# A graph layer, an attention over edges and four experts: one gather in 64 goes to another queue, and one pair is prepared a block earlier

## The chip, the cores and the metric

The kernel runs on one core of a Trainium2 chip. The core has engines with instruction streams of their own: TensorE (PE, with its weight load PEld), VectorE (DVE), ScalarE (ACT), GpSimd (POOL) and SyncE (SP). They order their work among each other by semaphores, which an instruction waits on and another raises. Data moves between HBM and the on-chip memory by DMAs, which POOL, SP and ACT issue. The metric is the device time of one execution in microseconds. The kernel before takes 6051.52 us (median of 3 runs, 6050.52 to 6075.12).

## The reference

Inputs are 12,500 nodes with 256 features, 200,000 edges sorted by their target, and a second list of 131,072 edges among 8,192 nodes that is not sorted. Two residual layers are computed, each on the normalised features:

```python
x = x + gnn(layernorm(x), src, dst, edge_weight, W, b)
x = x + ffn(layernorm(x)[None], W_gat, att_src, att_dst, b_gat,
            gamma, beta, W1, b1, W2, b2, edge_index)[0]

def gnn(features, src, dst, w, W, b):
    msgs = features[src] * w[:, None]
    agg = segment_sum(msgs, dst, num_segments=12500)      # dst is sorted
    return einsum('ni,oi->no', agg, W) + b

def ffn(x, ...):          # x: every node; 4 heads x 4 experts
    h = x @ W_gat
    alpha = softmax over the edges of each target (leaky_relu(a_src[src] + a_dst[dst]))
    scores = layernorm(segment_sum(h[src] * alpha) + b_gat).mean(heads)
    g = softmax of the two best experts' scores
    return sum over 4 experts of g[e] * (gelu(x @ W1[e] + b1[e]) @ W2[e] + b2[e])
```

The index lists are read on the chip; what depends on them (which step belongs to which tile) is worked out there.

## The kernel before

The program has three blocks, one after the other, with a barrier between them. The first (an opening, then `weighted_sums`) computes the first layer and ends near 3070 us. The second (`attention_and_experts`) runs the experts' products on TensorE while POOL and SP merge the sorted edges of the attention. The third combines the experts' results.

The change is in the first block, and at the seam to the second. In the first block the 200,000 edges lie as 1563 columns of 128 edges. Four columns are a **group** (GT = 4); there are 391 groups. The feature rows that the edges name are gathered from HBM into a **ring** of 16 slots (RING = 16), one group per slot, so that group g lies in slot g % 16. Sixteen groups are called a **round** here, r = g // 16; 24 rounds are full and seven groups are left over.

A gather is one indirect DMA of POOL, which brings one column: 128 rows of 1 KB (`gather`, line 692). The first 64 are issued in the opening (line 346, from the raw input). After that POOL runs through `refill(g)` for g = 16 to 390: it reads from `group_end` the step that ends group g - 16 (line 697), waits on `s_mm` until TensorE has done that step, and issues the four gathers of group g. POOL can so be at most 16 groups ahead of TensorE.

SP's loop (lines 673 to 676) waits for each slot until its four gathers have landed (`s_got[k]`, 16 per gather) and raises `s_ready`.

TensorE and VectorE work in **steps**, 488 in all, since a group whose edges belong to two output tiles is taken twice. VectorE makes four one-hot matrices of a step (`one_hots`: one TENSOR_SCALAR at line 916, four at line 920, each from the edges' targets and weights), two steps ahead of TensorE at most. TensorE waits for `s_hot` and `s_ready`, multiplies each with a gathered column into PSUM (`step`, line 861, four fp32 matmuls), and raises `s_mm`. When a step ends an output tile (98 tiles), TensorE also runs `stages` (lines 839 to 853), which with ScalarE takes the tile through W, the residual, the statistics and `W_gat`. Between the steps VectorE sorts the second edge list (for two thirds of the block), and TensorE counts and transposes for it.

Near the block's end VectorE computes the attention's node terms in two pieces: `terms(0)` for 88 tiles and `terms(1)` for the last ten, when all tiles are done.

In the second block the nodes are taken in 49 pairs of tiles. For a pair, ScalarE loads x (`load`, line 1276), VectorE normalises it (`normalise`, line 1421), TensorE transposes it (`turn`, line 1362), VectorE copies it out of PSUM (`out_of_psum`, line 1427), and then the experts' products start (line 1341). For pair 0 these stand in a row at the block's start.

Later in the second block SP fetches the attention's rows singly as well (line 1225, 80 bytes each), beside POOL's indirect gathers of the same table (line 1258).

## Time and profile before

| | |
|---|---|
| median of the runs (lowest, highest) | 6051.52 us (6050.52, 6075.12) |
| the profiled execution's own time | 6071.08 us |
| its span | 6069.4 us |
| TensorE busy | 3440.2 us (57% of the span) |
| POOL busy | 2688.8 us (44%) |
| VectorE busy | 2050.1 us (34%) |
| POOL's 1500 gathers of line 692 | 1432.4 us busy, 955 ns each |
| TensorE's 3904 matmuls of line 861 | 1171.9 us busy, 458 ns each |

The profile was taken in one execution; its own time is 0.3% above the median of the timed runs. "<-" in front of an engine and a name says what ended an idle time: a semaphore of that engine, a DMA, "remote" (a semaphore whose sender the profile doesn't resolve) or "issue" (the engine waited for nothing that the profile shows). PEclk is the clock that TensorE was granted, as a share of full speed.

### The profile page before, as it was taken

Reading aid. Unit: us, or ns where it says so; the run is one execution under the profiler, and the core shown is the slowest. Engines: PE = TensorE matmul, PEld = TensorE weight load, DVE = VectorE, ACT = ScalarE, POOL = GpSimd, SP = SyncE. Lnnn points to the kernel's source line nnn. Section 1 sums busy time; section 2 is a strip of 40 time slices with the busy share of each in tenths; the row PEclk is TensorE's granted clock in tenths of the full one; section 3 lists DMA queues with packets and bytes.
Section 4 is the critical chain, followed back from the end, with each engine's and each line's share of the span. In section 5 each row is a group of like instructions: output and inputs, shape, how many; then the busy total and the mean of one; then the engine's idle time right before and its main releaser. Section 6 shows DMA issues by size and latency. Waiting matters only on the chain. (4 is left out here: it accounts for less than half of the span.)

```text
span 6069.4 us, 66499 instructions
## 1 busy us (share of the span) xinstructions
PE 3440.2 (57%) x13893; PEld 2630.0 (43%) x13894; DVE 2050.1 (34%) x6854; ACT 818.5 (13%) x2321; POOL 2688.8 (44%) x2801
## 2 busy tenths in 40 slices
PE   1444535455556667677832224982928376389927
PEld 0333323333434545455621013871807255277826
DVE  5445454545453444423300000330303012033436
ACT  3100000000000111111200000220202011022216
POOL 4554545454444555555377774026070613420050
PEclk5666666676777777888955556995959688699968
DMA  7422222222222333333201101121111111111137
GB/s 236 130 81 64 74 61 73 70 75 66 73 64 77 91 89 95 89 96 96 71 15 10 13 11 20 60 78 14 56 14 40 28 35 43 19 50 44 55 124 304
DMA packets 281484, 425.60 MB, mean 70 GB/s; under 512 B 64296, under 2 KB 215091, under 8 KB 280243
## 3 DMA queue, kind: packets, MB, share of 16 engines
q0 software_dynamic: 113696, 216.93, 13.9%
q1 hardware_dynamic: 69567, 114.91, 5.2%
q10 hardware_dynamic: 98004, 91.50, 4.7%
q14 instruction: 157, 1.29, 0.1%
q8 instruction: 60, 0.98, 0.1%
HBM read 317.12 MB, written 105.98 MB: 70 GB/s over the span
## 5 line engine op out<-in xcount | busy, mean ns | idle before, releaser
L692 POOL DMA_INDIRECT rows<-feats,src_t x1500 | 1432.4, 955 | 1393.7 <-PE node_sums L861 817.6
L1258 POOL DMA_INDIRECT got<-row_dram,src_sorted x1008 | 995.4, 988 | 1313.0 <-DMA state_dram<-got 1005.1
L861 PE MATMUL node_sums<-rows,ys_ahead 128*128 x3904 | 1171.9, 458 | 709.8 <-issue 548.7
L861 PEld LDWEIGHTS node_sums<-rows,ys_ahead 128*128 128x128 f32 x3904 | 859.0, 230 | 992.7 <-issue 856.0
L1352 PE MATMUL d_expert<-w,hid 128*128 128x256 f32 x3136 | 806.3, 398 | 557.8 <-issue 553.2
L1341 PE MATMUL d_hidden<-d_yt,w 128*128 128x256 f32 x3136 | 807.6, 399 | 525.6 <-issue 518.9
L1352 PEld LDWEIGHTS d_expert<-w,hid 128*128 128x128 f32 x3136 | 624.9, 199 | 710.6 <-issue 629.2
L1341 PEld LDWEIGHTS d_hidden<-d_yt,w 128*128 128x128 f32 x3136 | 622.8, 200 | 676.9 <-issue 600.4
L1404 DVE TENSOR_TENSOR yo<-d_expert,x_and_b 128x512 f32<-128x512 f32 x196 | 135.6, 692 | 2169.4 <-remote 1124.4
L1285 ACT ACTIVATE hid<-d_hidden,b1c 128x256 f32<-128x256 f32 x784 | 324.0, 471 | 2312.4 <-remote 1091.6
L920 DVE TENSOR_SCALAR ys_ahead<-iota,rel,ew_t 128x128 f32<-128x128 f32 x1952 | 566.7, 361 | 117.9 <-issue 50.1
L916 DVE TENSOR_SCALAR rel<-dst_t,step_base 128x4 f32 x488 | 118.0, 242 | 1182.5 <-remote 597.8
L1038 DVE TENSOR_SCALAR ys_ahead<-iota_b,hist_columns 128x128 bf16<-128x128 bf16 (+1 forms) x2048 | 348.4, 267 | 106.2 <-issue 97.6
L751 ACT COPY edge_plan<-node_sums 128x256 f32<-128x256 f32 x98 | 36.5, 372 | 2555.9 <-remote 1700.1
L873 PE MATMUL counts<-ys_ahead 128*128 128x98 bf16 x1024 | 80.5, 251 | 254.4 <-DVEq L1041 184.5
L873 PEld LDWEIGHTS counts<-ys_ahead 128*128 128x128 bf16 x1024 | 68.8, 123 | 267.5 <-DVEq L1041 191.4
L1265 POOL DMA_INDIRECT first_row<-state_dram,first_end x1 | 0.9, 942 | 330.2 <-DMA state_dram<-got 330.2
L502 POOL DMA_INDIRECT adst_first<-node_dst,first_pos x98 | 96.0, 980 | 107.6 <-DVEq L1082 68.9
L1757 PE MATMUL f_sum<-ys,gate_diagonals 128*128 128x256 f32 x384 | 95.6, 413 | 75.1 <-issue 75.1
L849 PE MATMUL x_product<-edge_plan 128*128 128x256 f32 x400 | 129.2, 455 | 0.0
L833 PE MATMUL node_sums<-b_zeros 1*128 1x256 bf16 x198 | 59.3, 300 | 120.5 <-issue 105.9
L1757 PEld LDWEIGHTS f_sum<-ys,gate_diagonals 128*128 128x128 f32 x384 | 79.1, 209 | 91.2 <-issue 78.7
(303 smaller groups left out, 2473.2 us busy)
## 6 DMA issues: line engine op xcount, KB each, us to landing
y_dram<-yo ACTq DMA_DIRECT2D x196, 256.0 KB
ys<-y_dram SPq DMA_DIRECT2D x36, 1024.0 KB
got<-row_dram SPq DMA_DIRECT2D x2048, 0.1 KB
rows<-feats,src_t POOLq DMA_INDIRECT x1500
got<-row_dram,src_sorted POOLq DMA_INDIRECT x1008
ys_ahead<-y_dram SPq DMA_DIRECT2D x13, 1024.0 KB
x_dram<-edge_plan ACTq DMA_DIRECT2D x98, 128.0 KB
d_x<-x_dram ACTq DMA_DIRECT2D x49, 256.0 KB
```

The lines of the kernel that those rows point to most:

```text
L692: pool.indirect_dma_start(rows[:, g % RING, j, :], None, feats, bass.IndirectOffsetOnAxis(ap=m.src_t[:, g * GT + j:g * GT + j + 1], axis=0 ...
L849: t = pe.matmul(psX[:, 0:FEAT], sums_t[:, k * P:(k + 1) * P], w_t[:, k, :], start=False, stop=(k == HALVES - 1))
L861: t = pe.matmul(psA[:, ds(((code >> 1) & 1) * 512, FEAT)], hot[:, r, j, :], rows[:, ds((code >> 2) & (RING - 1), 1), j, :], start=False, s ...
L873: t = pe.matmul(psC[:, 0:TILES], hot_lo[:, q % 2, j, :], hot_hi[:, q % 2, j, :], start=False, stop=False)
L920: t = v.tensor_scalar(hot[:, r, j, :], m.iota[:], rel[:, r, j:j + 1], m.ew_t[:, ds(g * GT + j, 1)], ALU.is_equal, ALU.mult)
L1038: c.inc(v.tensor_scalar(t[:, q % 2, j, :], iota_b[:, 0:wide], col[:, q % 2, n, j:j + 1], None, ALU.is_equal))
L1258: pool.indirect_dma_start(got[:, k, j, 0:ROWF], None, m.row_dram, bass.IndirectOffsetOnAxis(ap=m.src_sorted[:, BEGIN[b] + j:BEGIN[b] + j + ...
L1285: t = act.activation(hid[:, e % 2, 2 * q + f, :], psL[(e % 2) * 2 + q][:, f, :], ACT.Gelu, bias=b1c[:, e, 2 * q + f:2 * q + f + 1])
L1341: t = pe.matmul(psL[(e % 2) * 2 + q][:, f, :], w1[:, h, e, (2 * q + f) * P:(2 * q + f + 1) * P], yt[:, k, h, :], start=(h == 0), stop=(h = ...
L1352: q = pe.matmul(psO[e % 2][:, t, :], hid[:, e % 2, f, t * P:(t + 1) * P], w2[:, f, e, :], start=(f == 0), stop=(f == FB - 1))
L1404: v.tensor_tensor(yo[:, e, :, :], psO[e % 2][:], xb[:, e, :, :], ALU.add).then_inc(s_yo, 1)
L1757: q = pe.matmul(psum[j % SUMS][:, t, :], diag[:, j % DIAGS, t, e, :], y_of(i)[:, t, e, :], start=(e == 0), stop=(e == EXPERTS - 1))
```

## The change

There are two edits.

**Rows.** In rounds 2 to 23, the fourth column (`ROW_COL` = 3) of slot 15 (`ROW_SLOT`) isn't gathered by POOL. SP loads that column's 128 node numbers and fetches the 128 rows one by one: ten after the ready signal of each slot from 2 to 13, and eight at slot 14. At slot 15 SP waits until all have landed. So that SP may write into the slot, POOL waits once a round, ahead of `refill(16r + 3)`, until TensorE has done group 16r - 1, and raises `s_free` (`row_slot_free`). `by_row` picks the group: with g = 16r + 3, g + 16 - 2 - 2 is 16r + 15.

**First pair.** x of pair 0 is loaded by ScalarE ahead of its work for tile 97, normalised by VectorE between `terms(0)` and `terms(1)`, transposed by TensorE after the first of the four closing stages and copied by VectorE. In the second block `load(0, 0)`, `normalise(0, 0)`, `turn(0)` and `out_of_psum(0, 0)` are gone, and the waits on their semaphores count one less.

```diff
+ROW_SLOT, ROW_COL, ROW_FROM, ROWS_A_GROUP = 15, 3, 2, 10
...
+        m.x_first, m.y_first = m.ys_ahead[:, HI_SLOT, 0, 0:2, :], m.ys_ahead[:, HI_SLOT, 0, 2:4, :]
+        m.yt_first = m.ys_ahead[:, HI_SLOT, 1, 0:2, :]
...
@@ weighted_sums, SP
+            def ask_nodes(i):
+                sp.dma_start(node_row_of, src_cols[ds(i * (RING * GT) + (ROW_SLOT * GT + ROW_COL), 1), :]
+                             ).then_inc(s_wr, 16)
+
+            def single_rows(a, z):
+                _, nodes = nc.values_load_multi_w_load_instructions(
+                    node_row_of[0:1, a:z], engines=[mybir.EngineType.SP], min_val=0, max_val=NODES - 1,
+                    skip_runtime_bounds_check_because="edge_index names nodes")
+                for n, node in enumerate(nodes):
+                    sp.dma_start(rows[a + n:a + n + 1, ROW_SLOT, ROW_COL, :], feats[ds(node, 1), :]
+                                 ).then_inc(s_rows, 16)
+
+            sp.wait_ge(s_wr, 16)
             with sp.Fori(2, full_rounds) as i:
+                ask_nodes(i)
                 for k in range(RING):
-                    sp.wait_ge(s_got[k], i * (16 * GT) + 16 * GT)
+                    if k == ROW_SLOT:
+                        sp.wait_ge(s_got[k], i * (16 * (GT - 1)) + (16 * GT + 16))
+                        sp.sem_inc(s_past, 1)
+                        sp.wait_ge(s_rows, i * (16 * P) - 16 * P)
+                    else:
+                        sp.wait_ge(s_got[k], i * (16 * GT) + 16 * GT)
                     sp.sem_inc(s_ready, 1)
+                    if k == ROW_FROM:
+                        sp.wait_ge(s_free, i)
+                        sp.sem_inc(s_past, 1)
+                        sp.wait_ge(s_wr, i * 16)
+                        sp.sem_inc(s_past, 1)
+                    a = (k - ROW_FROM) * ROWS_A_GROUP
+                    if 0 <= a < P:
+                        single_rows(a, min(a + ROWS_A_GROUP, P))
...
@@ weighted_sums, POOL
+            def by_row(g):
+                return g % RING == ROW_SLOT and 2 <= g // RING < full_rounds
+
             def gather(g):
                 for j in range(GT):
+                    if j == ROW_COL and by_row(g):
+                        continue
...
+            def row_slot_free(g):
+                end = pool.value_load(m.group_end[0:1, g - RING:g - RING + 1], min_val=1, max_val=STEPS)
+                pool.wait_ge(s_mm, end)
+                pool.sem_inc(s_free, 1)
...
             for g in range(RING, GROUPS):
+                if by_row(g + RING - ROW_FROM - 2):
+                    row_slot_free(g + RING - ROW_FROM - 2)
                 refill(g)
...
@@ weighted_sums, ScalarE
+                if j == TILES - 1:
+                    act.wait_ge(s_x1o[0], 16)
+                    act.wait_ge(s_x1o[1], 16)
+                    act.wait_ge(s_pos, 1)
+                    act.dma_start(m.x_first, m.x1_dram.rearrange("(t p) f -> t p f", p=P)[:, 0:2, :]
+                                  ).then_inc(s_xin, 16)
                 tile(j, j % XS)
...
@@ weighted_sums, TensorE: after stages(TILES)
+                    pe.wait_ge(s_turn, PIECES - 8)
+                    for t in range(2):
+                        for h in range(HALVES):
+                            q = pe.transpose(psT[:, h * N2 + t * P:h * N2 + (t + 1) * P],
+                                             m.y_first[:, t, h * P:(h + 1) * P], m.ident[:])
...
@@ weighted_sums, VectorE: after terms(0)
+                    v.wait_ge(s_xin, 16 * TILES + 16)
+                    for t in range(2):
+                        c.inc(v.tensor_scalar(m.y_first[:, t, :], m.x_first[:, t, :], m.mean[:, t:t + 1],
+                                              m.rstd[:, t:t + 1], ALU.subtract, ALU.mult))
...
+                    c.done(v.tensor_copy(m.yt_first, psT[:, 0:HALVES * N2].rearrange("p (h n) -> p h n", n=N2)))
...
@@ attention_and_experts
-            load(0, 0)
...
-            turn(0)
...
-            normalise(0, 0)
-            out_of_psum(0, 0)
```

On POOL, the place is the seam from group 34 to group 35 (the fourth group of round 2). Before, every group is one load of its `group_end`, one wait on TensorE's steps and four gathers:

```order
107 L697 TENSOR_LOAD group_end
108 L697 ISA x2
109 L692 DMA rows<-feats,src_t 128x256 [waits b_step_multiplied]
110 L692 DMA rows<-feats,src_t 128x256 x3
111 L697 TENSOR_LOAD group_end
112 L697 ISA x2
113 L692 DMA rows<-feats,src_t 128x256 [waits b_step_multiplied]
114 L692 DMA rows<-feats,src_t 128x256 x3
```

And in the changed kernel at the same place:

```order
107 L742 TENSOR_LOAD group_end
108 L742 ISA x2
109 L732 DMA rows<-feats,src_t 128x256 [waits b_step_multiplied]
110 L732 DMA rows<-feats,src_t 128x256 x3
111 L737 TENSOR_LOAD group_end
112 L737 ISA x2
113 L742 TENSOR_LOAD group_end [waits b_step_multiplied]
114 L742 ISA x2
115 L732 DMA rows<-feats,src_t 128x256 [waits b_step_multiplied]
116 L732 DMA rows<-feats,src_t 128x256 x3
```

A second load of `group_end` (line 737) and a wait now stand ahead of group 35's own. The second wait is for an earlier step than the first, and everything that POOL does later stands behind the first.

On SP, the place is the start of its loop over the rounds. Before, the loop body holds only waits and register work (the waits of all 16 slots are gathered into one row here, which is left out):

```order
54 L672 DMA state_dram<-edge_plan 128x24
55 L673 UNCONDITIONAL_BRANCH
56 L673 ISA
```

In the changed kernel it begins with the load of 128 node numbers, and from the third slot on each row is one instruction (ISA) that forms the address and one DMA:

```order
55 L694 UNCONDITIONAL_BRANCH [waits b_w_and_row_nodes_loaded]
56 L694 ISA
57 L682 DMA edge_plan<-in_src 1x128
58 L702 REGISTER_ALU
59 L707 REGISTER_ALU [waits rows_gathered0,rows_gathered1,rows_gathered2,x_cleared_then_row_slot_free]
60 L686 TENSOR_LOAD edge_plan [waits b_w_and_row_nodes_loaded]
61 L690 ISA
62 L690 DMA rows<-feats 1x256
63 L690 ISA
64 L690 DMA rows<-feats 1x256
```

SP's first row of a round stands behind the ready signals of slots 0 to 2 and behind POOL's signal `x_cleared_then_row_slot_free`; the ready signal of slot 3 stands behind ten rows.

On TensorE, the place is the seam of the blocks. Before, the second block opens with the transposes of pair 0:

```order
5313 L518 UNCONDITIONAL_BRANCH
5314 L1330 UNCONDITIONAL_BRANCH [waits barrier_Pool_Activation_PE_DVE_SP_release]
5315 L1362 MATMUL d_y_turned<-ident,d_y 128x128 [waits d_normed]
5316 L1362 MATMUL d_y_turned<-ident,d_y 128x128 x3
5317 L1341 MATMUL d_hidden<-d_yt,w 128x256 [waits d_yt_ready]
5318 L1341 MATMUL d_hidden<-d_yt,w 128x256 x15
```

In the changed kernel the transposes stand in the first block, between two of the closing stages, and the second block opens with the products:

```order
5301 L906 MATMUL sums_and_xc_turned<-ident,edge_plan 128x128 x2
5302 L964 MATMUL turned<-ident,ys_ahead 128x128 [waits b_turn_ask]
5303 L964 MATMUL turned<-ident,ys_ahead 128x128 x3
5304 L892 MATMUL h_product<-wg,edge_plan 128x16 [waits b_tile_out_of_psum]
...
5315 L521 UNCONDITIONAL_BRANCH
5316 L1398 UNCONDITIONAL_BRANCH [waits barrier_Pool_Activation_PE_DVE_SP_release]
5317 L1410 MATMUL d_hidden<-ys_ahead,w 128x256 x16
```

The experts' first products no longer wait for a transpose in their own block; the second of the closing stages stands behind a wait on VectorE.

## Rows read from the trace of the kernel before

**Rows 1.** Page, part 5: costliest groups in the first block (columns as the page's head says).
```profile
L692 POOL DMA_INDIRECT rows<-feats,src_t x1500 | 1432.4, 955 | 1393.7 <-PE node_sums L861 817.6
...
L861 PE MATMUL node_sums<-rows,ys_ahead 128*128 x3904 | 1171.9, 458 | 709.8 <-issue 548.7
```

**Rows 2.** Waits, whole span: engine, line, releaser: total us, times, longest us.
```profile
POOL rows L692 <- PE node_sums L861: 817.6, 96, 38.0
...
PE node_sums L861 <- issue: 548.7, 205, 13.3
...
PE node_sums L861 <- SPq L676: 27.6, 9, 3.8
```

**Rows 3.** Stretches of the first block: us; PE, PEld, DVE, ACT, POOL busy (instructions); PEclk; DMA; GB/s.
```profile
352.00:1936.00 1584.00, 799.96 (x3400) 582.75 (x3398) 790.75 (x3367) 72.75 (x290) 738.02 (x777) 0.69 0.24 70
1936.00:2958.00 1022.00, 729.01 (x2750) 521.86 (x2749) 391.43 (x1193) 144.29 (x580) 583.72 (x609) 0.83 0.32 93
2959.00:3028.00 69.00, 69.00 (x311) 52.48 (x312) 32.56 (x106) 18.50 (x74) 0.44 (x1) 0.96 0.10 30
```

**Rows 4.** One stretch, line 861 alone, then line 833 alone: PE, PEld, PEclk, DMA, GB/s.
```profile
2959.00:3028.00 69.00, 39.11 (x171) 32.05 (x172) 0.96 0.10 30
...
2959.00:3028.00 69.00, 4.28 (x15) 1.36 (x15) 0.96 0.10 30
```

**Rows 5.** POOL's timeline in one run of gathers: start, duration, line, [idle before <-releaser].
```profile
501.34 0.94 POOL L692 DMA_INDIRECT rows<-feats,src_t  x1 [26.40 <-PE node_sums L861]
502.58 0.97 POOL L692 DMA_INDIRECT rows<-feats,src_t  x1 [0.30 <-issue]
...
520.08 0.95 POOL L692 DMA_INDIRECT rows<-feats,src_t  x1 [0.31 <-issue]
```

**Rows 6.** Stretches within that run, all engines: columns as in rows 3.
```profile
501.00:508.00 7.00, 6.53 (x31) 5.40 (x29) 4.27 (x16) 0.00 (x0) 5.14 (x6) 1.00 0.28 78
508.00:521.00 13.00, 4.36 (x10) 2.35 (x8) 1.47 (x5) 0.00 (x0) 9.96 (x11) 0.61 0.39 110
```

**Rows 7.** Stretches in the opening: first gathers of the long run, the rest, behind it.
```profile
20.00:35.00 15.00, 5.55 (x25) 3.99 (x23) 14.30 (x53) 10.28 (x22) 11.35 (x12) 0.73 1.09 350
35.00:106.00 71.00, 5.64 (x8) 2.14 (x8) 16.45 (x63) 8.93 (x19) 48.78 (x51) 0.52 0.68 219
99.30:106.00 6.70, 0.00 (x0) 0.00 (x0) 2.93 (x9) 0.00 (x0) 0.00 (x0) 0.50 0.13 42
107.00:122.00 15.00, 0.00 (x0) 0.00 (x0) 14.48 (x76) 12.76 (x30) 0.00 (x0) 0.50 0.54 168
```

**Rows 8.** Stretches in the second block: start of a run of gathers, its rest, and without gathers.
```profile
4047.00:4062.00 15.00, 15.00 (x71) 13.19 (x71) 3.58 (x7) 1.68 (x4) 11.34 (x13) 1.00 0.84 315
4062.00:4235.00 173.00, 35.98 (x67) 17.61 (x65) 3.73 (x8) 3.36 (x8) 118.70 (x126) 0.52 0.11 12
4250.00:4350.00 100.00, 100.00 (x473) 88.05 (x472) 33.92 (x68) 29.27 (x61) 0.00 (x0) 1.00 0.15 50
```

**Rows 9.** SP's timeline in the second block, single rows: start, duration of all, count.
```profile
5634.29 134.34 SPq L1225 DMA_DIRECT2D got<-row_dram  x256
```

**Rows 10.** The same, beside POOL's gathers.
```profile
3149.92 179.90 SPq L1225 DMA_DIRECT2D got<-row_dram  x42
```

**Rows 11.** Timeline at the seam of the first two blocks.
```profile
3068.06 0.30 ACT L805 ACTIVATE std_all<-rstd_all,eps 128x10 f32<-128x10 f32 x1
...
3073.22 0.92 ACTq L1276 DMA_DIRECT2D d_x<-x_dram  x2
...
3076.11 0.73 DVE L1421 TENSOR_SCALAR d_y<-d_x,mean,rstd_all 128x256 f32<-128x256 f32 x2 [4.80 <-DMA d_x<-x_dram]
...
3076.90 1.11 PE L1362 MATMUL d_y_turned<-ident,d_y 128*128 128x128 f32 x4 [13.12 <-DVE d_y L1421]
...
3078.05 0.69 DVE L1427 COPY d_yt<-d_y_turned 128x512 f32<-128x512 f32 x1 [1.21 <-PE d_y_turned L1362]
...
3078.80 5.49 PE L1341 MATMUL d_hidden<-d_yt,w 128*128 128x256 f32 x12 [0.78 <-issue]
```

More of the change, by code:

```diff
@@ L169, in build @@
             opening = layernorm_and_plan(nc, sem, x, src, dst, edge_weight, feats, m)
-            weighted_sums(nc, sem, opening, feats, edge_index, x, W, b, W_gat, att_src, att_dst, W1, b1, W2, b2, m)
+            weighted_sums(nc, sem, opening, feats, src, edge_index, x, W, b, W_gat, att_src, att_dst, W1, b1, W2, b2, m)
         attention_and_experts(nc, sem, m)
@@ L503, in spread, with weighted_sums @@
                             m.node_dst[:, t, :], None).then_inc(m.s_sc, 16)
-def weighted_sums(nc, sem, opening, feats, edge_index, x, W, b, W_gat, att_src, att_dst, W1, b1, W2, b2, m):
+def weighted_sums(nc, sem, opening, feats, src, edge_index, x, W, b, W_gat, att_src, att_dst, W1, b1, W2, b2, m):
     XS = 4
@@ L571, in weighted_sums @@
         zeros = lent(512)
+        node_row_of = lent(P)[0:1, :].bitcast(I32)
         std = sb("std_all", [P, TILES])
@@ L585, in weighted_sums @@
         s_pc = sem("b_pool_const")
-        s_wr = sem("b_w_loaded")
+        s_wr = sem("b_w_and_row_nodes_loaded")
+        s_free, s_rows = m.s_clear, sem("b_rows_landed")
         s_w, s_wt, s_wte = sem("b_weights"), sem("b_w_turned"), sem("b_w_ready")
@@ L906, in _ @@
                 stages(d)
+                if d == TILES:
+                    pe.wait_ge(s_turn, PIECES - 8)
[3 more added lines that the diff above has]
+                                             m.y_first[:, t, h * P:(h + 1) * P], m.ident[:])
+                    q.then_inc(s_turned, 1)
         @block.vector
@@ L1333, in layer1 @@
             def layer1(i, k, n, e, first=False):
-                if e == 0:
-                    pe.wait_ge(s_yt, i + 1)
+                turned = m.yt_first if isinstance(i, int) and i == 0 else yt[:, k]
+                if e == 0 and not (isinstance(i, int) and i == 0):
+                    pe.wait_ge(s_yt, i)
                 for q in range(2):
@@ L1356, in turn @@
             def turn(i):
-                pe.wait_ge(s_yn, i + 1)
-                if not isinstance(i, int) or i >= 1:
-                    pe.wait_ge(s_yt, i)
+                pe.wait_ge(s_yn, i)
+                if not isinstance(i, int) or i >= 2:
+                    pe.wait_ge(s_yt, i - 1)
                 for t in range(2):
@@ L1410, in x_and_b2 @@
                 bias = b2p[:, e, :] if e < IN_PSUM else b2r[:, e, :]
-                v.tensor_tensor(xb[:, e, 0, :], xd[:, k, 0, :], bias, ALU.add).then_inc(s_xh, 1)
+                of = m.x_first if isinstance(i, int) and i == 0 else xd[:, k]
+                v.tensor_tensor(xb[:, e, 0, :], of[:, 0, :], bias, ALU.add).then_inc(s_xh, 1)
                 v.wait_ge(s_xh, i * EXPERTS + (e + 1))
-                v.tensor_tensor(xb[:, e, 1, :], xd[:, k, 1, :], bias, ALU.add).then_inc(s_xb, 1)
+                v.tensor_tensor(xb[:, e, 1, :], of[:, 1, :], bias, ALU.add).then_inc(s_xb, 1)
             def normalise(i, k):
-                v.wait_ge(s_x[k], (i // 2) * 16 + 16 if isinstance(i, int) else i * 8 + (16 - 8 * k))
-                if not isinstance(i, int) or i >= 1:
-                    v.wait_ge(s_ty, i)
+                v.wait_ge(s_x[k], (i // 2) * 16 + 16 * k if isinstance(i, int) else i * 8 + 8 * k)
+                if not isinstance(i, int) or i >= 2:
+                    v.wait_ge(s_ty, i - 1)
                 for t in range(2):
```

12 lines of the change are left out of this document (9 added, 3 removed).

## The prediction

> **What bounds the kernel now.** I read the page's costliest groups first. POOL's gathers of the first block take 1432.4 us, and POOL is idle nearly as long before them, most of it released by TensorE's matmul of line 861 [rows 1]. The table of waits says the same from both sides: POOL waits 817.6 us for TensorE, TensorE only 27.6 us for SP's ready signal, in nine waits [rows 2]. So POOL is ahead by the whole ring, and the rows that it fetches are in time. The wait row to look at is TensorE's "issue": 548.7 us in 205 pieces of up to 13.3 us [rows 2], in which nothing that the profile shows holds it. The question is what does.
>
> The answer is in the stretches around POOL's runs of gathers. In one run POOL starts 16 gathers from 501.34 to 520.08, one every 18.74 / 15 = 1.25 us [rows 5]. In the first 7 us of it the other engines issue 31 + 29 + 16 instructions; in the 13 us after that, with the gathers still running, 10 + 8 + 5 [rows 6]. That is 10.9 per us against 1.8. The opening's long run has it too: after its first dozen gathers, 8 + 8 + 63 + 19 = 98 instructions come in 71 us (1.4 per us), and TensorE has none in the 6.7 us after the last gather; then VectorE alone issues 76 in 15 us [rows 7]. In the second block, TensorE has 71 matmuls in the first 15 us of such a run (the whole of which it is busy), then 67 in 173 us, and 473 in 100 us without gathers [rows 8]. Granted clock and issue fall together there (1.00 to 0.52), but half the clock can't explain a seventh of the instructions. So I read: a run of gathers back to back leaves the other engines alone for about 8 gathers (10 us), then slows all of them to 0.86 (148 in 173 us, rows 8) to 1.8 instructions per us until some 7 us after its end. Short runs cost little; long ones cost nearly their whole length.
>
> In this sense the ring's fullness before is a good thing: since POOL is always 16 groups ahead, it gets a slot only when TensorE has done a group, and its runs stay at 8 to 16 gathers by my count along its timeline, of which rows 5 are one.
>
> **The change, part by part.**
>
> *Fewer gathers.* 22 of 1500 gathers go; 22 x 1.25 = 27 us less for POOL, which waits 817.6 us anyway [rows 1, 2]. By itself I count this as nothing to at most 27 us.
>
> *POOL's new wait.* Ahead of group 16r + 3 POOL waits until TensorE has done group 16r - 1. Its own wait there is for group 16r - 13. So once a round POOL's lead falls from 13 to 16 groups to three (16r to 16r + 2). Behind the waiting instruction stand all of POOL's later gathers; SP's ready signals stand behind these. Once TensorE is there, the slots of groups 16r + 3 to 16r + 15 are free together: 13 x 4 - 1 = 51 gathers without a wait, and 12 more (the next three groups) that want TensorE to have done 16r to 16r + 2. POOL then runs 63 gathers in one go, 63 x 1.25 = 78.7 us, where before 64 came in four to six runs. With the 6.7 us behind it [rows 7] this is 85.4 us.
>
> How far does TensorE get in them? The instructions per group come from the two parts of the block: 777 gathers are 194 groups, with (3400 + 3398 + 3367 + 290) / 194 = 54 instructions on the four engines; later, when the sort is over, 609 are 152 groups, with 7272 / 152 = 48 [rows 3]. In the first 10 us it runs undisturbed, 2.1 groups at the pace below. In the remaining 69 us to the last gather I take 0.86 per us, the nearest row that had SP's single rows beside it: 59 instructions, 1.1 groups. Together 3.2 groups, just what it takes for POOL to issue its last 12 gathers without a stop. The bounds: nothing in the slow part (2.1 groups), or 1.8 per us (2.5 groups, 4.6 together).
>
> The undisturbed pace is read where POOL has gathered its last: from 2959 to 3028 line 861 has 171 records; 3904 over 488 steps are 8 a step, so 21.4 steps. Line 833 has 15, two a tile, so 7.5 tiles end there, each of which makes one step more than there are groups: 13.9 groups [rows 1, 4]. Of the 69 us I take off 7 for the run's tail: 62 / 13.9 = 4.46 us per group late in the block. Early on there are 54 instructions instead of 48 for each: an estimate of 5.0 us, above VectorE's 790.75 / 194 = 4.1 us of work per group [rows 3].
>
> A round after the change is then 85.4 + 12.8 x 5.0 = 149.4 us early and 85.4 + 12.8 x 4.46 = 142.5 us late. Before it is 1584 / 777 x 64 = 130.5 and 1022 / 609 x 64 = 107.4 [rows 3]. Rounds 2 to 13 lie in the early part, 14 to 23 in the late one: 12 x 18.9 + 10 x 35.1 = 227 + 351 = +578 us. As a test of the rule, a round before with some 33 us of slow time in it gives 33 + 16 x 4.46 = 104 late (107.4 measured), and 113 early (130.5): early it may be 17 us too kind.
>
> *SP's rows.* Without gathers beside it SP issues 256 single rows in 134.34 us, 0.525 us each [rows 9]; beside them 42 in 179.90 us, 0.23 per us [rows 10]. The rows here are 1 KB and not 80 bytes, which no row of before shows. In the first 10 us of a run some 15 rows go out, in 69 us at 0.23 another 16; the 97 left take 51 us in the quiet part, which has 57 (late) to 64 us (early). So they are hidden, by a little; the ready signal of slot 15 is the first to be late if a row costs over 0.66 us (64 / 97) early, or 0.59 late. I take nothing here and keep the dearer case as a rival. Below nothing it can't be: these are instructions added.
>
> *The first pair.* At the seam ScalarE's load is issued at 3073.22, VectorE normalises at 3076.11, TensorE transposes at 3076.90 and its products start at 3078.80 [rows 11]. Without these four steps the products could start when the load did, 5.6 us earlier. Against it the closing stages wait for two normalisations and four transposes (0.73 + 1.11 us in rows 11), beside work that ends at 3068.06. Between +3 and -6 us; I take -5.
>
> The sum: 578 - 5 = +573, on the profiled execution's 6071 us 6644. That execution was 20 us above the median of the runs, so I forecast 6051.5 + 573 = 6625 us.
>
> **Bounds of the likeliest case.** With 4.6 groups in the run, rounds of 11.4 groups: 142.4 and 136.2, 12 x 11.9 + 10 x 28.8 = +431, 6480. With 2.1 groups: 154.9 and 147.4, +693, 6740; and with the 17 us that the early rounds lacked, 6740 + 204 = 6940. I take 6350 to 6900 as its own range.
>
> **Rivals.**
>
> 1. *Slow, but in shorter runs.* TensorE hasn't done group 16r when POOL has issued 51 gathers; POOL stops, and the last 12 go out four at a time, as before. A round is 51 x 1.25 + 6.7 = 70.5 us with three groups, and 13 groups: 135.5 and 128.5, 12 x 5.0 + 10 x 21.1 = +271: 6320, down to 6100 if the pause sets in earlier. For it: 3.2 groups are near. Against it: two of the three groups it asks for are done in the undisturbed 10 us. 0.10.
>
> 2. *Dearer: SP's rows are the bound.* If a 1 KB row costs 0.8 us when quiet, 97 take 78 us, and a round is 85 + 78 = 163: 12 x 32.5 + 10 x 55.6 = +946, 7000. It decides from 0.6 us a row. Against it: rows 9. 0.07.
>
> 3. *No change.* The gathers and the slow stretches only happen to fall together, POOL's 4 x 1.25 = 5.0 us per group stay below TensorE's 107.4 / 16 = 6.7 us, and a lead of three groups is enough. Then only the first pair counts: 6046. For it: POOL waits 817.6 us. Against it: three stretches of different kinds show the same fall [rows 6 to 8]. 0.06. The Trainium skill (SBUF — State Buffer, Who interferes with whom) would have this one: it says that only the port pair that VectorE and GpSimd share makes engines wait for each other, so that TensorE would go on beside any run of gathers. TensorE's 67 matmuls in 173 us beside gathers against 473 in 100 us without [rows 8] speak against that rule, whatever the carrier.
>
> 4. *Faster.* One long run per round leaves a long quiet stretch; place: TensorE's pace between POOL's runs. It decides by how many groups TensorE does in the 85.4 us: the round is shorter than before from 16 - (130.5 - 85.4) / 5.0 = 7.0 groups early, and 16 - (107.4 - 85.4) / 4.46 = 11.1 late. With one group more than that in each round, 12 x 5.0 + 10 x 4.5 = 105 us are gained: 5945. For it: nothing but that the short runs, too, have a slow part each. Against it: TensorE would need two to three times what rows 6 show. 0.06.
>
> **How the numbers follow.** The forecast has 0.71, the rivals 0.10, 0.07, 0.06 and 0.06. The range 6130 to 6900 leaves out rivals 2 to 4 (0.19). A measurement of this kernel can tell about 0.5% (30 us) from no change: faster 0.06, the same 0.06, slower 0.88.
>
> **What would show it.** In the profile after, POOL's timeline in rounds 2 to 23 has runs of about 60 gathers and then an idle time of some 60 us that TensorE's matmul ends; before the change the longest of these was 38.0 us [rows 2]. TensorE's and VectorE's "issue" waits grow by some hundreds of us, PEclk in the first block falls, and the block ends near 3640 us instead of 3070, with the second and third as long as before. The first-pair step is right if the experts' products start within some 2 us of ScalarE's first work in their block. The forecast is wrong if TensorE's pace within POOL's long runs is like that outside of them, or if it is TensorE's wait on SP's ready signal that has grown.

## The result, and the profile after

The changed kernel takes 6998.04 us (median of 4 runs, 6990.66 to 7002.02), the kernel before 6058.89 us on the same chip: a ratio of 1.155 (95% interval 1.1528 to 1.1573), 939 us more. The forecast was 6625 us in a range of 6130 to 6900. The direction was right; the size was not, and the time lies outside the range.

The whole difference is in the first block. By the times at which TensorE finishes groups (my own count from its matmuls), round 23 ends at 3930.8 us instead of 3002.2 and round 1 ends 29 us earlier than before (323.2, 352.0). From the experts' first products to the end it is 2990.5 us, as before (2990.6). The page after, its line of engines and the two groups that answer to [rows 1]:

```profile
PE 3482.9 (50%) x13893; PEld 2631.6 (38%) x13894; DVE 2034.7 (29%) x6854; ACT 819.6 (12%) x2321; POOL 2659.6 (38%) x2779
...
L732 POOL DMA_INDIRECT rows<-feats,src_t x1478 | 1410.3, 954 | 2327.1 <-issue 2049.3
L914 PE MATMUL node_sums<-rows,ys_ahead 128*128 x3904 | 1220.7, 469 | 1438.9 <-issue 610.1
```

Busy times are nearly as before; what has grown is idle time. TensorE is busy 43 us longer, at a lower granted clock (0.64 and 0.70 in the stretches below, 0.69 and 0.83 in [rows 3]), so the clock is a small part of the 939 us. The table of waits, to be read beside [rows 2]:

```profile
POOL rows L732 <- issue: 2049.3, 1455, 95.9
...
PE node_sums L914 <- issue: 610.1, 198, 40.3
PE node_sums L914 <- remote: 353.8, 18, 39.9
PE node_sums L914 <- SPq L703: 352.4, 88, 26.4
```

Three things are to be seen. POOL's waits are put down to "issue", since the second load of `group_end` now stands between the wait and the gather; its 21 pieces above 10 us, 1612 us together and up to 95.9 us long, are the new wait (own count); the rest are the short gaps between gathers. TensorE's pieces of "issue" are up to 40.3 us long instead of 13.3. And there is a wait that was almost absent: TensorE for SP's ready signal, 352.4 us in 88 pieces instead of 27.6 us in nine. Of the 353.8 us whose sender the profile doesn't resolve ("remote"), 306 us end with an update of the same ready semaphore (own count), so the wait is nearer 650 us.

Rounds 2 to 13 and 14 to 23, from round end to round end, all engines (columns as in [rows 3]):

```profile
323.20:2312.50 1989.30, 790.20 (x3399) 574.74 (x3398) 786.93 (x3365) 74.16 (x295) 721.45 (x756) 0.64 0.19 55
2312.50:3930.80 1618.30, 836.94 (x2943) 573.79 (x2942) 397.15 (x1258) 155.07 (x622) 615.57 (x646) 0.70 0.22 64
```

The 756 gathers are 12 x 63. A round takes 1989.3 / 12 = 165.8 us early and 1618.3 / 10 = 161.8 us late; by the same marks it took 132.0 and 106.7 before. So +33.8 and +55.1 us, 12 and 10 times: 957 us. Early and late rounds are now nearly as long as each other, although the early ones have the sort beside them: whatever sets the round hardly depends on TensorE's and VectorE's work any more.

One late round shows it. First POOL's timeline of the round that begins near 2788 (columns as in [rows 5]), its gathers in the middle left out:

```profile
2789.98 1.02 POOL L732 DMA_INDIRECT rows<-feats,src_t  x1 [81.94 <-issue]
2791.31 0.95 POOL L732 DMA_INDIRECT rows<-feats,src_t  x1 [0.30 <-issue]
...
2869.02 0.94 POOL L732 DMA_INDIRECT rows<-feats,src_t  x1 [0.30 <-issue]
2950.72 1.02 POOL L732 DMA_INDIRECT rows<-feats,src_t  x1 [80.76 <-issue]
```

One run from 2790 to 2870, then 80.76 us of nothing. SP's single rows of the same round, asked for in three stretches (start, duration, line, count):

```profile
2791.23 7.36 SPq L690 DMA_DIRECT2D rows<-feats  x10
...
2797.89 75.78 SPq L690 DMA_DIRECT2D rows<-feats  x19
...
2877.17 60.42 SPq L690 DMA_DIRECT2D rows<-feats  x100
```

(One row counts in two of the stretches at the seam.) Ten rows go out at once, 18 more in the 76 us beside the run and in its tail, 4.2 us apart in most of it by SP's own starts, and then 100 in 60.42 us. The last stands at 2937.6, about 149 us after the round's start.

Why is a row ten times dearer beside the gathers? On SP a row is three instructions: two that only form its address in registers (FUSED_REGOPS, MOVE) and the DMA. One of the address instructions, in a stretch of the run and in the quiet stretch (count: shortest/median/longest in ns, first and last start):

```profile
L690 SPq MOVE rows<-feats x16: 17/700/711, 2801.4 to 2863.9; - x16
...
L690 SPq MOVE rows<-feats x95: 3/29/37, 2878.6 to 2935.7; - x95
```

All three have a median of 700 ns in the run; two of them move no data. They start 1.40 us apart, and another engine's instruction starts halfway between (VectorE's at 2821.19, 2822.60 and 2824.00, SP's at 2821.87, 2823.27 and 2824.67). So it is not the transfer that is dear: the issue of instructions, SP's and the others' alike, has come down to one per 0.70 us.

TensorE at the round's end:

```profile
2935.58 0.76 PE L914 MATMUL node_sums<-rows,ys_ahead 128*128 x2
2939.27 3.67 PE L914 MATMUL node_sums<-rows,ys_ahead 128*128 x8 [2.93 <-SPq L703]
...
2947.37 4.94 PE L914 MATMUL node_sums<-rows,ys_ahead 128*128 x22
```

TensorE waits 2.93 us for SP, and then has slot 15, a tile's end and the steps up to the next gate to do: the next run starts at 2950.72, 13 us after the last row. In all 22 rounds the last row stands 145 to 163 us after the round's start (own count; about 150 on average), and the round ends 4 to 32 us later, 13 to 14 on average.

### The profile page after: what moved, and what is told of

It reads as the page before. It is cut to its first block and busy times, and to the rows that moved or that the text cites. A ratio compares the mean times of both kernels' runs of the same rounds, so it can differ in the third digit from the quotient of the medians.

```text
span 6993.1 us, 75480 instructions
## 1 busy us (share of the span) xinstructions
PE 3482.9 (50%) x13893; PEld 2631.6 (38%) x13894; DVE 2034.7 (29%) x6854; ACT 819.6 (12%) x2321; POOL 2659.6 (38%) x2779
## 5 line engine op out<-in xcount | busy, mean ns | idle before, releaser
L732 POOL DMA_INDIRECT rows<-feats,src_t x1478 | 1410.3, 954 | 2327.1 <-issue 2049.3
L914 PE MATMUL node_sums<-rows,ys_ahead 128*128 x3904 | 1220.7, 469 | 1438.9 <-issue 610.1
L1410 PE MATMUL d_hidden<-d_yt,w 128*128 128x256 f32 x3072 | 779.6, 396 | 473.1 <-issue 468.7
L1410 PEld LDWEIGHTS d_hidden<-d_yt,w 128*128 128x128 f32 x3072 | 605.2, 198 | 614.5 <-issue 541.6
L980 DVE TENSOR_SCALAR ys_ahead<-iota,rel,ew_t 128x128 f32<-128x128 f32 x1952 | 550.7, 347 | 98.8 <-issue 24.1
L798 ACT COPY edge_plan<-node_sums 128x256 f32<-128x256 f32 x98 | 36.5, 373 | 3482.9 <-PE sums_and_xc_turned L906 2124.4
L1098 DVE TENSOR_SCALAR ys_ahead<-iota_b,hist_columns 128x128 bf16<-128x128 bf16 (+1 forms) x2048 | 352.0, 255 | 179.9 <-issue 170.7
L1094 DVE CAST hist_columns<-ys_ahead 128x16 f32<-128x16 bf16 x128 | 16.4, 177 | 317.7 <-remote 185.9
```

The lines of the kernel that those rows point to most:

```text
L732: pool.indirect_dma_start(rows[:, g % RING, j, :], None, feats, bass.IndirectOffsetOnAxis(ap=m.src_t[:, g * GT + j:g * GT + j + 1], axis=0 ...
L914: t = pe.matmul(psA[:, ds(((code >> 1) & 1) * 512, FEAT)], hot[:, r, j, :], rows[:, ds((code >> 2) & (RING - 1), 1), j, :], start=False, s ...
L980: t = v.tensor_scalar(hot[:, r, j, :], m.iota[:], rel[:, r, j:j + 1], m.ew_t[:, ds(g * GT + j, 1)], ALU.is_equal, ALU.mult)
L1098: c.inc(v.tensor_scalar(t[:, q % 2, j, :], iota_b[:, 0:wide], col[:, q % 2, n, j:j + 1], None, ALU.is_equal))
L1410: t = pe.matmul(psL[(e % 2) * 2 + q][:, f, :], w1[:, h, e, (2 * q + f) * P:(2 * q + f + 1) * P], turned[:, h, :], start=(h == 0), stop=(h ...
```

## The experiments

The changed kernel has two parts that can cost: POOL's early wait, with the long run that it makes, and SP's rows. Four kernels take these apart; all but the third have the first pair in them. They ran on a slower chip than the first comparison (the kernel before took 6114.88 us there), so ratios are what is compared.

**The wait alone.** POOL gathers all 64 columns and SP's loop is as before; the wait stays.

```diff
                 for j in range(GT):
-                    if j == ROW_COL and by_row(g):
-                        continue
                     pool.indirect_dma_start(rows[:, g % RING, j, :], None, feats,
...
```

> The changed kernel without the single rows: POOL gathers all 64 columns of a round and keeps the new wait ahead of group 16r + 3. Theory: the loss of the change has two parts, TensorE's slow stretch during the one long run of gathers, and SP's single rows, whose last lands some 150 us into each round, whatever TensorE does. Without the rows a round is 85 us (run and tail) with 4.2 (early) to 4.9 (late) groups done, then 11.8 x 5.0 or 11.1 x 4.46 us: 144 and 135 us instead of 132 and 107, so 12 x 12 + 10 x 28 = +424 us, about 6480 us (6380 to 6600). Rival A, the long run harms nobody and the rows are the whole loss: within 30 us of 6055. Rival B, the rows are hidden and the long run is the whole loss: 6990.

Measured: 6688.42 us, ratio 1.0934 (1.0916 to 1.0952), +574 us. Neither rival. Rounds 2 to 13 and 14 to 23:

```profile
328.80:2179.80 1851.00, 763.07 (x3399) 547.42 (x3398) 786.16 (x3364) 73.97 (x295) 730.58 (x768) 0.65 0.20 59
2179.80:3623.30 1443.50, 788.69 (x2943) 543.09 (x2942) 399.05 (x1258) 154.68 (x622) 623.07 (x656) 0.70 0.25 71
```

That is 154.3 and 144.4 us a round. The prediction's rule for the long run had said 149.4 and 142.5 and +578 us; the expectation before this run, which took 1 to 2 more groups in the run from the changed kernel's trace, was some 150 us too low. TensorE's waits here are mostly "issue", 909.2 us in 292 pieces, with little on SP:

```profile
PE node_sums L883 <- issue: 909.2, 292, 20.5
...
PE node_sums L883 <- SPq L682: 18.5, 1, 18.5
```

**The rows alone.** POOL's signal is given where its own refill waits for the same step, so nothing is waited for early.

```diff
-                if by_row(g + RING - ROW_FROM - 2):
-                    row_slot_free(g + RING - ROW_FROM - 2)
+                if by_row(g):
+                    row_slot_free(g)
```

> The changed kernel with POOL's signal moved from ahead of group 16r + 3 to ahead of group 16r + 15, whose own refill waits for the same step: POOL keeps its lead and its short runs, SP still fetches 128 rows a round between its ready signals. Theory: the rows pace TensorE even so: 128 rows at 0.58 us with the loads between are 74 us, some 10 us until the first and 12 us after the last, and 20 to 30 us in which gathers run and rows come four times slower or worse: 115 to 125 us a round, against 132 early and 107 late, so about 6100 to 6250 us. Rival A (the rows are the whole loss): 6990. Rival B (the long run is the whole loss): 6030 to 6060.

Measured: 6502.96 us, ratio 1.0639 (1.0621 to 1.0658). POOL has its short runs again (at most 16 gathers without a stop of 1.5 us in rounds 2 to 23), yet rounds are 143.1 and 133.7 us and the last row stands at about 125 us in each part of the block (own count). The theory had the kind of loss right and its size too small by half or more (+388 us, where it had +42 to +192). TensorE waits 502.9 us for SP's ready signal (line 703). So the rows set the round by themselves, at a lower level. The two losses alone, 9.3% and 6.4%, add up to 15.7%, nearly the 15.5% of the whole change.

**The first pair alone.** The second edit on the kernel before.

```diff
+                if j == TILES - 1:
...
+                    act.dma_start(m.x_first, m.x1_dram.rearrange("(t p) f -> t p f", p=P)[:, 0:2, :]
+                                  ).then_inc(s_xin, 16)
...
-            load(0, 0)
...
-            turn(0)
...
-            normalise(0, 0)
-            out_of_psum(0, 0)
```

> The kernel before with only the second edit: the first pair is loaded, normalised and turned in the first block; no rows by SP, no new wait of POOL. Theory: 5 us less than before, 6050 to 6056 where before is 6058, hard to tell from no change. Rival: the closing stages, held by the wait on VectorE, give the time back or more: 6058 to 6064.

Measured: 6117.81 us, ratio 0.9999 (0.9987 to 1.0011). No change that can be told by the times; the interval is wider than the 5 us. The traces tell a little more: from the first of the four closing stages to the experts' first products it takes 41.3 us before, 36.5 in the changed kernel and 38.4 here (one execution each). In the changed kernel the products start within 0.03 us of ScalarE's load, and the four transposes stand between two closing stages without a wait ahead of them:

```profile
3971.36 1.06 PE L964 MATMUL turned<-ident,ys_ahead 128*128 128x128 f32 x4
...
3972.46 0.69 DVE L1180 COPY ys_ahead<-turned 128x512 f32<-128x512 f32 x1 [10.22 <-PE turned L964]
...
4002.63 0.40 ACTq L1345 DMA_DIRECT2D d_x<-x_dram  x1
...
4002.66 9.63 PE L1410 MATMUL d_hidden<-ys_ahead,w 128*128 128x256 f32 x32 [6.70 <-PEq L521]
```

**Half the rows.** The wait, and 64 of the 128 rows, five between two ready signals; the other 64 are left out.

```diff
-ROW_SLOT, ROW_COL, ROW_FROM, ROWS_A_GROUP = 15, 3, 2, 10
+ROW_SLOT, ROW_COL, ROW_FROM, ROWS_A_GROUP, ROWS_IN_ALL = 15, 3, 2, 5, 64
...
```

> The changed kernel with only the first 64 of the 128 rows fetched, five between two ready signals (the other 64 rows keep what an earlier round left there, so the sums of these columns are not the reference's). Theory: 22 rows are out when the long run ends, the other 42 take 25 us, less than TensorE's 50 to 59 us that are left, so SP no longer sets the round and the time is that of the kernel with the wait alone, within 40 us. Rival: each row costs in proportion, because SP's instructions take TensorE's places or the transfers collide: halfway between the kernel with the wait alone and 6998.

Measured: 6696.12 us, ratio 1.0951 (1.0929 to 1.0972), the same as the wait alone within 10 us. 64 rows cost nothing and the other 64 cost 6% of the kernel, so a row has no price of its own. The last of the 64 stands 115 us after the round's start on average, and TensorE takes 35 us more to end the round (own count): what counts is whether SP's rows, and the ready signals between them, come later than TensorE's own work.

The next three ask why a long run costs, and whether it must. POOL gets one or three short memsets behind each gather and waits for their end before it goes on. The first two are made from the kernel before:

```diff
                                             ).then_inc(s_got[g % RING], 16)
+                    if g >= 2 * RING:
+                        for _ in range(1):
+                            c.done(pool.memset(pause[:], 0.0))
```

(`pause` is 128 x 128; the second has `range(3)`.)

> The kernel before with one memset of 128 x 128 (about 0.2 us, and a wait for its end) on POOL behind each of its gathers from round 2 on; nothing else. The question is whether the other engines are slowed because gathers follow each other without a pause. Theory (something that a gather leaves behind piles up when they come every 1.25 us, and is worked off when they come a little slower): at about 1.5 us per gather a round of 64 takes POOL 96 us; with little or no slow time rounds fall from 132 and 107 us to about 100 and 98, that is 12 x 32 + 10 x 9 = some 470 us less, a ratio of 0.92 (0.90 to 0.97). Rival (the gathers slow the others whatever the pause between them, once several have been issued): rounds get longer by the pause in the runs, 64 x 0.25 = 16 us at most, a ratio of 1.00 to 1.06.

Measured: ratio 0.9672 (0.9656 to 0.9688), 5860.55 against 6056.84 us, at the slow end of what was expected. The kernel before becomes faster by giving POOL more to do. "Issue" before TensorE's matmuls falls from 548.7 us to 45.0, and what is left is a wait for rows:

```profile
PE node_sums L865 <- SPq L677: 492.3, 142, 5.3
...
PE node_sums L865 <- issue: 45.0, 36, 10.7
```

> The same with three memsets behind each gather (about 2.1 us from gather to gather). Theory: POOL needs 64 x 2.1 = 134 us for a round and sets it, with TensorE and VectorE undisturbed and waiting for rows: 134 us early (as before) and 134 instead of 107 late, 10 x 27 = +270 us, a ratio of 1.03 to 1.06, and TensorE's idle time is a wait on SP's ready signal, not issue. Rival (slowing whatever the pause): 134 us of gathers with the others at a third of their pace, rounds of 150 us and more: a ratio of 1.11 or more.

Measured: ratio 1.093 (1.0912 to 1.0948): POOL sets the round, more strongly than the theory had it (144.9 us early and 146.1 late by my count, where it had 134), and TensorE's "issue" is 28.5 us, its wait for SP 1135.9 us. The kind is as expected, the size was not: the gap with the group's own load is 1.35 us where POOL has waited, which I hadn't counted.

The same three memsets on the kernel with the wait alone:

> The kernel with POOL's new wait alone (all 64 gathers, no single rows) with three memsets behind each gather from round 2 on. Theory: the long run of 63 gathers takes 132 us instead of 79, but the other engines keep their pace in it, so TensorE follows POOL and a round is 132 us and the few groups that TensorE is behind at its end, about 135 to 145 us, against 154 and 144 with the wait alone: a ratio to the kernel before of 1.04 to 1.08, less than 1.09 although POOL works longer. Rival: the run of 132 us slows the others for its whole length: rounds of 132 + 7 + 50 = 190 us, a ratio of 1.20 or more.

Measured: ratio 1.0961 (1.0943 to 1.0979), above the expectation for the same reason. Beside the pause without the wait (1.093), the early wait costs 0.3% with the pause and 9.3% without it. That doesn't show a wait that is harmless by itself: with three memsets POOL is slower than TensorE and has no lead to lose, and from round 3 on it stands at the gate for 2.0 to 2.3 us a round, against 35 to 100 us in the kernel with the wait alone (own count). So these two kernels run nearly alike, and whether the wait costs something where POOL has a lead is not shown here. That it is the unbroken run that is dear rests on the stretches above, on the next kernels, and on the last two, in which the whole change, wait and all, costs 0 and 3.5% beside pauses instead of 15.5%.

How short must the runs be? The pause behind each fourth gather, each second, each eighth and each sixteenth, and a tiny memset (128 x 1) behind each, all on the kernel before. The edit for each fourth (for each second the condition is `j % 2 == 1`; for each eighth and sixteenth `g % 2 == 1` and `g % 4 == 3` are added):

```diff
+                    if g >= 2 * RING and j == GT - 1:
+                        c.done(pool.memset(pause[:, 0:P], 0.0))
```

> The kernel before with one memset of 128 x 128 (0.24 us) and a wait for its end on POOL after the fourth gather of each group only, from round 2 on. Theory: runs of four never reach the eight gathers after which the others were slowed; a group takes POOL 4 x 1.25 + 0.24 + 1.35 (the group's own load, as measured beside the pause) = 6.3 to 6.6 us, 101 to 106 us a round instead of 113 to 118 with the pause behind each gather: a ratio of 0.92 to 0.95. Rival (it must be a pause behind every gather, since what piles up needs that time): rounds near those before, a ratio of 0.98 to 1.02.

> The same behind every second gather. Theory: 4 x 1.25 + 2 x 0.24 + 1.35 = 6.8 us a group, 109 us a round, between the pause by group and the pause by gather: a ratio of 0.94 to 0.96. Rival, as for the pause by group: 0.98 or more.

> The kernel before with a memset of 128 x 1 (some 0.1 us instead of 0.24) and a wait for its end behind each gather. It tells whether the length of the pause matters or that POOL waits for an own instruction before it issues the next gather. If the wait does it: as fast or a little faster than with 0.24 us, 0.95 to 0.97. If the length does it (less than half the time for what piles up): 0.98 to 1.00.

> The kernel before with the pause after each second group only, so that runs have eight gathers. Theory (the slowing sets in after about eight gathers without a pause): 8 x 1.25 + 1.6 = 11.6 us for two groups, 93 us a round instead of 101.5, 22 x 8.5 = 190 us less than with the pause by group: a ratio of 0.89 to 0.91. If the slowing sets in earlier or the pause after eight is too short to end it: 0.93 or more.

> The kernel before with the pause after each fourth group, runs of at most sixteen gathers. Theory: the second half of each run slows the others, some 10 us four times a round and 2 us behind each, so rounds are between 100 and 120 us: a ratio of 0.95 to 1.00, worse than with eight. If it isn't the length of the run but POOL's waiting that matters: 0.87 to 0.90, better than with eight.

The last column counts the sign that SP's rows showed above: register instructions of TensorE, VectorE, ScalarE and SP in rounds 2 to 23 that last 0.68 to 0.72 us, of some 13,100 with a median of 0.046 us (own count).

| pause behind | ratio | 95% interval | rounds early, late (us) | held for 0.70 us |
|---|---|---|---|---|
| none (kernel before) | 1 | | 132.0, 106.7 | 845 |
| each gather, 0.24 us memset | 0.9672 | 0.9656 to 0.9688 | 111.4, 112.0 | 0 |
| each gather, 0.11 us memset | 0.9384 | 0.9368 to 0.9400 | 105.0, 103.7 | 2 |
| each second | 0.9388 | 0.9372 to 0.9404 | 104.7, 105.0 | 1 |
| each fourth | 0.9267 | 0.9251 to 0.9282 | 101.7, 101.4 | 7 |
| each eighth | 0.9667 | 0.9643 to 0.9691 | 122.2, 99.6 | 606 |
| each sixteenth | 0.9886 | 0.9858 to 0.9914 | 130.6, 100.9 | 692 |

The best lies at four: 5624.29 us, 7.3% under the kernel before. Pauses in more places make POOL the bound; fewer bring the slow stretches back (TensorE's "issue" at line 864 is 48.3 us with four, 335.1 with eight, 488.8 with sixteen). In the early rounds eight gathers are too many already, against the theory of that run: either the slowing sets in earlier, or the pause behind eight is too short to end it. Late in the block eight cost no time, although instructions are held there too. A memset of half the length does better, so a longer pause isn't what is needed. Whether it is the wait for an own instruction, or only the slower pace that it makes, these runs don't separate: a gather takes 1.57 us on average with the pause behind four (6.29 / 4), about 1.45 behind eight by the expectation's sum (11.6 / 8), and 1.25 in an unbroken run. POOL's timeline with the pause by group:

```profile
999.90 0.97 POOL L693 DMA_INDIRECT rows<-feats,src_t  x1 [1.35 <-PE node_sums L864]
1001.17 0.95 POOL L693 DMA_INDIRECT rows<-feats,src_t  x1 [0.30 <-issue]
1002.43 0.94 POOL L693 DMA_INDIRECT rows<-feats,src_t  x1 [0.30 <-issue]
1003.68 0.95 POOL L693 DMA_INDIRECT rows<-feats,src_t  x1 [0.30 <-issue]
1004.62 0.23 POOL L697 MEMSET edge_plan<- 128x128 f32 x1
1006.19 0.95 POOL L693 DMA_INDIRECT rows<-feats,src_t  x1 [1.34 <-PE node_sums L864]
```

A group takes 1006.19 - 999.90 = 6.29 us and 16 of them 101 us, which is the measured round. Without the pause the gap before a group's first gather is the same 0.30 us as between any two once POOL's run is going (0.31 before the fifth of the run in [rows 5], at 506.36); with it, 1.35.

Last, the change with such pauses: is it then harmless, or a gain?

```diff
+                    if g >= 2 * RING:
+                        c.done(pool.memset(pause[:, 0:P], 0.0))
```

(In the changed kernel, behind each gather, 64 x 128; in the second the two lines stand behind the loop over a group's gathers.)

> The changed kernel (single rows, new wait, first pair) with one memset of 64 x 128 and a wait for its end on POOL behind each gather from round 2 on. Theory: both parts of the loss come from gathers that follow each other without a pause, which slow TensorE and SP alike. With the pause SP issues its 128 rows in about 75 us from some 10 us on, inside POOL's 63 paced gathers of about 111 us, and the early wait costs nothing: a ratio to the kernel before of 0.96 to 0.98, as for the kernel before with the same pause, although nothing of the change is undone. Rival A (the rows are dear in themselves, whatever POOL does): 150 us a round remains, a ratio above 1.08. Rival B (the rows set the round at 100 to 120 us): 1.00 to 1.05.

Measured: 0.9668 (0.9652 to 0.9685), the kernel before with a pause of 128 x 128 in the same places being 0.9672 (111.4 and 112.0 us a round): the change costs and brings nothing there, with rounds of 114.0 and 111.1 us.

> The changed kernel with one memset of 64 x 128 and a wait for its end on POOL after the last gather of each group, from round 2 on. Theory: undisturbed SP needs 5.8 us for ten rows and POOL 6.3 us for a group, so the rows follow POOL and cost nothing: as the kernel before with the same pause, a ratio of 0.92 to 0.94. Rival A (the rows set the round once POOL is not the slower one): the last row lands at 85 to 100 us and 12 us follow, rounds of 105 to 112 us, a ratio of 0.94 to 0.97. Rival B (the rows are dear in themselves): 1.00 or more.

Measured: 0.9619 (0.9588 to 0.9649) against 0.9267 without the change, rival A. SP's timeline shows one round whole:

```profile
2068.96 0.23 SPq L683 DMA_DIRECT2D edge_plan<-in_src  x1
2083.08 96.98 SPq L691 DMA_DIRECT2D rows<-feats  x128
2184.15 0.23 SPq L683 DMA_DIRECT2D edge_plan<-in_src  x1
```

From one load of node numbers to the next it is 115.2 us: 14 until the first row, 97 for 128 rows, 4 behind them. With the gathers broken up, rounds are 111 to 114 us and the change costs 3.5% of the kernel. The last row stands 93 to 108 us after the round's start and the round ends 4 to 29 us later (own count), so I take the rows for the bound that is left. No run has the wait with this pause and without rows; POOL stands at the gate for up to 25.9 us here, so a part of the 3.5% could be the wait's. Nor is the slow issue wholly gone: 289 register instructions are held for 0.70 us (1525 in the changed kernel without pauses).

## Why the prediction was wrong

**What bounds the kernel, and the long run: right.** TensorE is held by runs of gathers, not by missing rows; POOL's wait joins the runs to one of 63; its price was forecast at +578 us, and the kernel with the wait alone shows +574. That the two agree so closely is in part luck, as three parts of the sum were off and made up for each other. TensorE does more than 3.2 groups in most of the runs (3.1 to 4.8 in the changed kernel's runs of 63, 4.5 on average in the long runs of the wait alone, by my marks). Behind the run its pace is slower than the prediction had it, 6.1 us a group early and 4.9 late in the kernel with the wait alone instead of 5.0 and 4.46. And the onset is earlier than eight gathers: in the kernel before, the first register instruction that is held for 0.70 us comes 4 to 8 gathers into a run, six as a rule, and in the changed kernel, with SP's rows beside it, 2 to 7 (own count, for runs that follow at least 15 us without gathers). One reading of [rows 8] was too mild: 67 in 173 us against 473 in 100 us is a twelfth of the pace and not a seventh.

**The step that failed: "SP's rows ... So they are hidden, by a little ... I take nothing here."** They cost 1.155 - 1.093 of the kernel, some 370 us. I compared 97 rows at 0.525 us (51 us) with TensorE's 57 to 64 us, and the three numbers of that comparison each leaned the same way. 28 rows and not 31 were out before the quiet stretch, which begins some 8 us behind the last gather. The other 100 took 60.42 us, 0.60 each: 0.41 from row to row within ten, and up to 2.8 between tens, where the loads of the node numbers and a ready signal stand (SP's own starts). And behind the last row TensorE still had 13 us to do before the next gate, which I had set on TensorE's side of the comparison as if it could run beside the rows. 79 + 8 + 60 + 13 = 160 us, within 1 us of that round. The comparison was of two amounts of work; it should have been of two chains with a seam.

Nor is the signal of slot 15 the first to be late, as the prediction has it. Every signal from slot 3 on stands behind rows, ten as a rule. In the quiet stretch of the round shown SP raises eleven of them from 2878.6 to 2938.7, 6.0 us apart, where TensorE's undisturbed group takes 4.46 us; TensorE waits for SP ahead of slots 7, 9, 10, 12, 14 and 15 (own reading). The prediction named this as a sign that it is wrong: "if it is TensorE's wait on SP's ready signal that has grown".

**The rival that came true** is the second: SP's rows as the bound, 7000 us from rounds of 163. The measured rounds are 165.8 and 161.8. That its time is met within 2 us is luck: it has 97 rows at 0.8 us, 78 us, where the runs show 100 at 0.60 us and 13 us behind them, 73 us, and a tail that is longer by 1 to 2 us. It had 0.07 because I asked for a dearer row; none was needed. Its point of decision, 0.59 us a row late in the block, was too high for the same reason as above: without the 13 us of the seam, TensorE's 57 us leave 44 for 100 rows, 0.44 us each, which the 0.525 us of [rows 9] exceeds.

**The rivals "no change" and "faster"** fall with the wait alone (1.0934). "Shorter runs" happened in seven of the 22 rounds (51 and 59 gathers), but those rounds aren't shorter for it: 168 us from gate to gate on average against 162 (own count, the last round aside).

**The first pair:** within its bounds, too small to be told by the times; the traces of four kernels that have it show 2.1 to 4.8 us less at the seam.

**What stays open** is the carrier. The runs show that the other engines' issue is held at one instruction per 0.70 us while POOL issues indirect gathers without a pause, and freed where it waits after every four; POOL's own register instructions are never held so long (152 ns at most in rounds 2 to 23). Neither the load on the DMA engines nor the fetch of instructions is in sight there: in 172 us of the slow stretch of the second block that [rows 8] shows, the DMAs move 12 GB/s, and none of their packets belongs to a queue of instructions:

```profile
DMA packets 4926, 2.09 MB, mean 12 GB/s; under 512 B 2142, under 2 KB 4926, under 8 KB 4926
...
q0 software_dynamic: 4032, 1.30, 9.1%
q10 hardware_dynamic: 816, 0.79, 1.4%
q1 hardware_dynamic: 78, 0.00, 0.0%
```

What is shared was not tried. Every time here comes with the profiler's record of that execution, so no run shows whether instructions are held as long without it.

## What to carry to other kernels

When a wait collapses a producer's lead, ask what the producer does when it is let go: a burst can cost more than the wait. A transfer moved to an idle queue is hidden only if its last piece, and what must follow it before the next round can start, fits in the round; and a piece's price here is that of its instructions, not of its bytes (0.525 us for 80 bytes in [rows 9], 0.60 for 1 KB, 4.2 for the same 1 KB beside the run). And a queue that is never waited for may be too fast for its neighbours: a pause after every four gathers brought 7.3%, where this change brought nothing.

## What the runs showed that I had not expected

Indirect gathers every 1.25 us slow the other engines' issue, and the same gathers with a wait for a 0.1 us memset behind them, 1.33 us apart within a group, don't: TensorE's idle "issue" fell from 548.7 us to 45.0 with 0.24 us behind each gather (60.2 with 0.1 us). In the slow stretches even an instruction that only moves a register takes 0.70 us, against 0.03 us otherwise. The gap before a group's first gather, in which POOL's load of `group_end` stands, is 1.35 us behind such a wait and 0.30 us without one.
